# V stationary, the softmax's division in the transposing product, groups masked by one minimum

## What is computed

```python
x = x + xattn(layernorm(x), ctx, Wq, Wk, Wv, Wo, bo)
#   4 heads of 64: attn = softmax(q k^T / 8); (attn v) Wo^T + bo
x = x + ffn(layernorm(x), ...)
#   gate: scores = softmax(xf gw + gb), 32 experts in 8 groups of 4
#   a group's score is the sum of its 2 best; the 4 best groups stay,
#   the rest is masked; the 4 best experts of what stays get the token
#   routed experts (256 -> 128 -> 256, silu) and one shared expert
```

## Time and profile before

| | us |
|---|---|
| median of three runs | 429.52 |
| the three runs | 429.52, 421.88, 429.8 |
| the profiled execution | 428.41 |
| its span, first to last instruction | 426.6 |
| mean granted TensorE clock | 0.935 of full speed |
| PE, DVE, ACT, POOL busy | 343.8, 276.8, 183.5, 169.6 |

### The profile page before, as it was taken

One profiled execution on the slowest core, in us unless ns is written; L12 is line 12 of the kernel. 1 busy time (PEld: TensorE's weight loads), 2 busy tenths in 40 slices (PEclk: granted clock), 3 DMA queues, 4 the chain that ended last, 5 costly groups with the idle time before them and its releaser, 6 DMA issues.

```text
span 426.6 us, 8875 instructions
## 1 busy us (share of the span) xinstructions
PE 343.8 (81%) x2356; PEld 293.2 (69%) x2356; DVE 276.8 (65%) x906; ACT 183.5 (43%) x621; POOL 169.6 (40%) x197
## 2 busy tenths in 40 slices
PE   4889999999999899989697888889888778885000
PEld 3687988888879787768586866778777666673000
DVE  4736697786978869795423665556655565564297
ACT  2384675666657644441123444444444344342000
POOL 3702005362543625664300644554554534554000
PEclk9987999999999999997888999999999999999555
DMA  7992617557316412132121454554454534531699
GB/s 238 347 367 77 209 51 276 183 201 247 118 61 224 169 47 94 47 98 113 64 76 37 153 151 141 163 154 140 149 153 151 161 115 142 158 115 65 249 412 347
DMA packets 34277, 68.95 MB, mean 162 GB/s; under 512 B 5323, under 2 KB 25836, under 8 KB 33356
## 3 DMA queue, kind: packets, MB, share of 16 engines
q1 hardware_dynamic: 27292, 47.54, 35.0%
q0 software_dynamic: 6960, 21.11, 13.3%
HBM read 39.87 MB, written 28.77 MB: 161 GB/s over the span
## 4 chain that ended last, share of the span: by engine, by line
PE 43%; DVE 20%; issue 12%; ACT 7%; DMA 5%; DVEq 4%; another core or an unknown queue 4%; ACTq 2%; SPq 1%; POOL 0%; POOLq 0%
PE psS L1105 10%; PE psF L905 4%; PE psG L1114 3%; PE psS L1096 3%; PE psS L87 3%; PE psF L87 3%; DVEq L117 3%; DMA hs_ctx<-in_ctxT 2%; DVE nmax L1169 2%; PE psF L1114 2%; PE psF L1004 2%; DVE w L1565 2%; DVE xn2T_all L1553 2%; DMA w<-shares 2%
## 5 line engine op out<-in xcount | busy, mean ns | idle before, releaser
L609 POOL DMA_INDIRECT shares<-xn2T_all,e_number x81 | 84.0, 1036 | 104.3 <-DVE xn2T_all L1553 86.2
L568 POOL DMA_INDIRECT dispatch<-work,slot_now x64 | 62.4, 975 | 91.4 <-issue 47.8
L1105 PE MATMUL psS<-work,arena 128*128 128x128 f32 x648 | 87.6, 279 | 3.1 <-DVE arena L1548 2.8
L1105 PEld LDWEIGHTS psS<-work,arena 128*128 128x128 f32 x648 | 79.9, 194 | 4.8 <-DVE arena L1548 3.8
L1542 DVE SCALAR_TENSOR_TENSOR work<-psS,b,work 128x128 f32<-128x128 f32 x81 | 28.3, 349 | 62.0 <-issue 38.6
L806 ACT ACTIVATE work<-psS 128x256 f32<-128x256 f32 x81 | 30.9, 383 | 60.5 <-PE psS L1096 27.7
L1548 DVE COPY arena<-w 128x768 f32 x81 | 44.8, 554 | 6.7 <-PE psG L1114 2.9
L817 ACT ACTIVATE work<-psS,b 128x128 f32<-128x128 f32 x81 | 29.6, 366 | 36.9 <-PE psS L1105 34.1
L1114 PE MATMUL psG<-arena,work 128*128 128x256 f32 x80 | 25.9, 406 | 16.4 <-DVE work L1542 12.1
L1096 PE MATMUL psS<-ident,xn2T_all 128*128 128x128 f32 x162 | 31.8, 279 | 3.3 <-issue 1.5
L905 PE MATMUL psF<-arena 128*128 128x64 f32 x256 | 32.4, 282 | 1.3 <-ACT arena L682 1.3
(11 more groups left out here) (213 smaller groups left out, 754.7 us busy)
## 6 DMA issues: line engine op xcount, KB each, us to landing
xn2T_all<-dispatch SPq DMA_DIRECT2D x81, 160.0 KB
w<-in_w SPq DMA_DIRECT2D x6, 1536.0 KB, 8.4
w<-shares SPq DMA_DIRECT2D x7, 1024.0 KB, 11.2
dispatch<-padding SPq DMA_DIRECT2D x8, 640.0 KB
w<-in_w SPq DMA_DIRECT2D x1, 2304.0 KB, 8.0
out<-x SPq DMA_DIRECT2D x7, 256.0 KB, 10.1
hs_ctx<-in_ctxT SPq DMA_DIRECT2D x8, 192.0 KB, 3.4
x<-in_x SPq DMA_DIRECT2D x1, 1536.0 KB, 10.1
```

What stands on the lines that cost most here:

```text
L568: pool.indirect_dma_start(dispatch, bass.IndirectOffsetOnAxis(ap=slot_now[:, par, j * TOPK + k:j * TOPK + k + 1], axis=0), xn2[:, par, j, ...
L609: pool.indirect_dma_start(shares, bass.IndirectOffsetOnAxis(ap=e_number[:, u:u + 1], axis=0), e_y[:, u, :], None).then_inc(added[u], 16)
L1105: ins = pe.matmul(psS[:, 2 + u % 2, m * P:(m + 1) * P], e_w13[:, u % 3, k, m * INTER:(m + 1) * INTER], e_xT[:, u % 3, k, :], start=(k == 0 ...
```

## The change

The division by the row sums moves from behind the attention to before it. DVE makes, for each j, `scaling`: 4 diagonal blocks of 128 x 128, the identity times the reciprocals of one head's row sums. The product that turns the probabilities takes it in the identity's place, so pT comes out divided. attend then has V stationary (64 columns of it) and both j's pT as 256 moving columns; it writes the transposed result at once, the two heads of a bank half on two sets of partitions, the one on partitions 0 to 63, the other on 64 to 127. attend_T and attend_take are gone, and exps is split by j. `scaling` has one buffer: product 1 waits for probs_T 0. The router's keep, keep1 and two mask operations become `bound` = 7 - 2 rank and a minimum with the score. The order of the calls changes on PE, ACT and DVE, and the scatter is paced by other semaphores.

```diff
 def step(b, par, tail2):
     if tail2:
-        last_one = isinstance(b, int) and b == BATCHES - 1
-        scatter(b - 2, par, (("att_psum", TPB * (b + 1)),
-                             ("proj_psum", TPB * b + 1) if last_one else ("scores_psum", TPB * (b + 2)),
-                             ("proj_psum", TPB * (b + 1) if last_one else TPB * b + 1)))
+        last_two = isinstance(b, int) and b >= BATCHES - 2
+        last_one = last_two and b == BATCHES - 1
+        scatter(b - 2, par, (("attT_psum", b + 1) if last_one else ("scores_psum", TPB * (b + 2)),
+                             ("proj_psum", TPB * b + 1),
+                             ("proj_psum", TPB * (b + 1)) if last_two else ("q_psum", b + 3)))
 split_context(1, 1)
 step(0, 0, False)
...
-        ins.then_inc(s["probs_ready"], 1)
+def exps(b, j):
+    act.wait_ge(s["nmax_ready"], TPB * b + (j + 1))
+    for hp in range(HEADS):
+        ins = act.activation(probs[:, j, hp, :], psS[:, 2 * j + hp // 2, (hp % 2) * LQ:(hp % 2 + 1) * LQ], ACT.Exp,
+                             bias=nmax[:, j, hp:hp + 1], accum_out=psums[:, j, hp:hp + 1])
+    ins.then_inc(s["probs_ready"], 1)
 def gate_exps(b):
     act.wait_ge(s["gate_max"], b + 1)
...
     if front:
         q_out(b + 1)
         k_out(b + 1)
+    probs_out(b, 0)
+    if front:
         v_out(b + 1, 1 - par)
-    probs_out(b, 0)
     probs_out(b, 1)
     if tail:
         norm2_out(b - 1)
     if front2:
         round_context(b + 2, par, nth)
-    if tail:
-        gate_exps(b - 1)
-        norm2_keep(b - 1)
-    if front2:
         norm(b + 2)
     if not front:
+        if tail:
+            gate_exps(b - 1)
+            norm2_keep(b - 1)
         for c in range(WHOLE, 6):
             round_chunk(c)
         silu(0, 0)
         silu(0, 1)
     attend_out(b)
-    if not front:
+    if front:
+        exps(b + 1, 0)
+        if front2:
+            norm_out(b + 2)
+        if tail:
+            gate_exps(b - 1)
+            norm2_keep(b - 1)
+        exps(b + 1, 1)
+    else:
         silu(1, 0)
         silu(1, 1)
-    if front2:
-        norm_out(b + 2)
-    if front:
-        exps(b + 1)
 def norm2_out(b):
     act.wait_ge(s["xn2T_psum"], b + 1)
...
     if j == 0:
         pe.wait_ge(s["q_ready"], b + 1)
         pe.wait_ge(s["k_ready"], b + 1)
+        if not (isinstance(b, int) and b == 0):
+            pe.wait_ge(s["pT_ready"], TPB * (b - 1) + 1)
     for h in range(HEADS):
         r = HD * (h % 2)
         ins = pe.matmul(psS[:, 2 * j + h % 2, (h // 2) * LQ:(h // 2 + 1) * LQ], qT[r:r + HD, h // 2, j * P:(j + 1) * P],
...
     ins.then_inc(s["scores_psum"], 1)
 def probs_T(b, j):
-    pe.wait_ge(s["probs_ready"], TPB * b + (j + 1))
+    pe.wait_ge(s["scaling_ready"], TPB * b + (j + 1))
     for t in range(2):
         for hp in range(HEADS):
-            ins = pe.transpose(psS[:, 2 * j + t, hp * P:(hp + 1) * P], probs[:, j, hp, t * P:(t + 1) * P], ident[:, :])
+            ins = pe.matmul(psS[:, 2 * j + t, hp * P:(hp + 1) * P], probs[:, j, hp, t * P:(t + 1) * P], scaling[:, hp, :],
+                            start=True, stop=True)
     ins.then_inc(s["pT_psum"], 1)
-def attend(b, j, par, front):
-    pe.wait_ge(s["pT_ready"], TPB * b + (j + 1))
+def attend(b, par, front):
+    pe.wait_ge(s["pT_ready"], TPB * (b + 1))
     pe.wait_ge(s["v_ready"], b + 1)
     if front:
-        pe.wait_ge(s["q_ready" if j == 0 else "k_ready"], b + 2)
-    elif j == 1:
+        pe.wait_ge(s["k_ready"], b + 2)
+    else:
         pe.wait_ge(s["x1_ready"], TPB * b)
-    for hp in range(HEADS):
-        h = (hp % 2) * 2 + hp // 2
+    for k in range(KD):
+        y = psF[:, 1, k * LQ:(k + 1) * LQ].rearrange("p (j q) -> p j q", j=TPB)
         for t in range(2):
-            ins = pe.matmul(psF[:, 2 - j, h * HD:(h + 1) * HD], pT[:, j, t, hp, :], v_sb[:, par, t, h * HD:(h + 1) * HD],
-                            start=(t == 0), stop=(t == 1))
-    ins.then_inc(s["att_psum"], 1)
-def attend_T(b, front):
-    for j in range(TPB):
-        pe.wait_ge(s["att_ready"], TPB * b + (j + 1))
-        if front and j == 0:
-            pe.wait_ge(s["v_ready"], b + 2)
-        for k in range(KD):
-            ins = pe.transpose(attT_bank(b)[:, j * LQ + k * P:j * LQ + (k + 1) * P], att[:, j, k * P:(k + 1) * P], ident[:, :])
+            for r in range(2):
+                h, rows = 2 * k + r, slice(r * HD, (r + 1) * HD)
+                ins = pe.matmul(y[rows], v_sb[:, par, t, h * HD:(h + 1) * HD], pT[:, :, t, 2 * r + k, :],
+                                start=(t == 0), stop=(t == 1))
     ins.then_inc(s["attT_psum"], 1)
-def project(b):
+def project(b, front):
     pe.wait_ge(s["attT_ready"], b + 1)
+    if front:
+        pe.wait_ge(s["v_ready"], b + 2)
     for j in range(TPB):
         pe.matmul(proj_bank(b, j), part_rows[0:PARTS[-1] + 1, :], bo_parts[0:PARTS[-1] + 1, :], start=True, stop=False)
         for k in range(KD):
-            ins = pe.matmul(proj_bank(b, j), attT[:, j, k, :], wo[:, k, :], start=False, stop=(k == KD - 1))
+            ins = pe.matmul(proj_bank(b, j), attT[:, k, j * P:(j + 1) * P], wo[:, k, :], start=False, stop=(k == KD - 1))
         ins.then_inc(s["proj_psum"], 1)
 def norm2_T(b, par):
...
     if front:
         proj_q(b + 1)
         proj_k(b + 1, 1 - par)
+    probs_T(b, 0)
     if front:
         proj_v(b + 1, 1 - par)
-    probs_T(b, 0)
-    if not front:
+    else:
         pe.wait_ge(s["x1_ready"], TPB * (b - 1) + 1)
         shared_up(0, 0)
+    probs_T(b, 1)
     if tail2 and front:
         ranks(b - 2)
-    probs_T(b, 1)
     if not front:
         pe.wait_ge(s["pT_ready"], TPB * b + 1)
         shared_up(0, 1)
         ranks(b - 2)
     if tail:
         norm2_T(b - 1, 1 - par)
-    attend(b, 0, par, front)
+    if front:
+        scores(b + 1, 0)
+    attend(b, par, front)
     if tail:
         gate(b - 1)
-    attend(b, 1, par, front)
-    if front:
-        scores(b + 1, 0)
-    else:
-        shared_up(1, 0)
-    attend_T(b, front)
     if front:
         scores(b + 1, 1)
     else:
+        shared_up(1, 0)
         shared_up(1, 1)
     if front2:
         norm_T(b + 2)
-    project(b)
+    project(b, front)
 pe.wait_ge(s["wk_in"], 16)
 proj_k(0, 0)
...
-    dve.tensor_scalar(keep1[:, :, :], grank[:, :, :], TOPG - 0.5, 1.0, ALU.is_lt, ALU.subtract).then_inc(s["groups_kept"], 1)
+    dve.tensor_scalar(bound[:, :, :], grank[:, :, :], -2.0, 2.0 * TOPG - 1.0, ALU.mult, ALU.add).then_inc(s["groups_kept"], 1)
 def route_mask(b):
     dve.wait_ge(s["groups_kept"], b + 1)
-    st.did(dve.tensor_tensor(by_group(masked), by_group(score), spread(keep[:, :, :].rearrange("p t g -> p (t g)"), 2, GSIZE), ALU.mult), "kept")
-def route_others(b):
-    st.need("kept")
-    dve.tensor_tensor(by_group(masked), by_group(masked), spread(keep1[:, :, :].rearrange("p t g -> p (t g)"), 2, GSIZE),
-                      ALU.add).then_inc(s["masked_ready"], 1)
+    dve.tensor_tensor(by_group(masked), by_group(score), spread(bound[:, :, :].rearrange("p t g -> p (t g)"), 2, GSIZE),
+                      ALU.min).then_inc(s["masked_ready"], 1)
 def route_best(b):
...
     st.need("rows")
     dve.tensor_copy(slot_now[:, par, :], row_now[:, :, :].rearrange("p t k -> p (t k)")).then_inc(s["slots_ready"], 1)
-def attend_sums(b):
-    dve.wait_ge(s["probs_ready"], TPB * b + TPB)
-    st.did(dve.reciprocal(prcp[:, :, :], psums[:, :, :]), "prcp")
-def attend_take(b, j):
-    st.need("prcp")
-    dve.wait_ge(s["att_psum"], TPB * b + (j + 1))
-    dve.tensor_tensor(att[:, j, :].rearrange("p (h l d) -> p l h d", l=2, d=HD),
-                      psF[:, 2 - j, 0:D].rearrange("p (h l d) -> p l h d", l=2, d=HD),
-                      spread(prcp[:, j, :].rearrange("p (l h) -> p l h", l=2), 3, HD), ALU.mult).then_inc(s["att_ready"], 1)
+def attend_sums(b, j):
+    dve.wait_ge(s["probs_ready"], TPB * b + (j + 1))
+    st.did(dve.reciprocal(prcp[:, j, :], psums[:, j, :]), f"prcp{j}")
+def attend_scaling(b, j):
+    st.need(f"prcp{j}")
+    if not (isinstance(b, int) and b == 0 and j == 0):
+        dve.wait_ge(s["pT_psum"], TPB * b + j)
+    dve.tensor_tensor(scaling[:, :, :], spread(ident[:, :], 1, HEADS), spread(prcp[:, j, :], 2, P), ALU.mult).then_inc(s["scaling_ready"], 1)
 def rows_of(b, j):
     return x[:, ds(TPB * b + j, 1), :].rearrange("p a d -> p (a d)")
...
             residual(b, j)
         wait_apart(dve, s["x1_ready"], TPB * b + (j + 1))
         dve.bn_stats(st2[:, j, :], rows_of(b, j)).then_inc(stats_ready[j], 1)
-    if tail:
-        route_others(b - 1)
+    if attended:
+        attend_sums(b + 1, 0)
     for j in range(TPB):
         wait_apart(dve, stats_ready[j], nth)
         ins = dve.bn_aggr(mv2[:, j, :], st2[:, j, :])
...
         route_best(b - 1)
     st.need("aggr")
     rsqrt_var(n, mv2[:, :, 1])
+    if attended:
+        attend_scaling(b + 1, 0)
     if tail:
         route_index(b - 1)
     rsqrt_half(n)
...
         route_onehot()
     newton_wyy(n, tmp)
     newton_root(n, tmp)
```

(43 more changed lines are left out.)

8 lines of the change are left out of this document (1 added, 7 removed).

## The result

The changed kernel takes 451.69 us (median of 4 runs, 448.85 to 454.29), the kernel before on the same chip 428.52 (4 runs): ratio 1.063, 95% interval 1.046 to 1.081. Times are medians of all executions; ratios compare undisturbed executions alone, so that a ratio isn't exactly the quotient of two medians. The change makes the kernel slower, as forecast, but by 23 us and not by 9, and it lies above the whole range.

What follows compares the result with a forecast made beforehand. DVE's chain of waits, not PE, bounds the attention steps. 6.85 (five middle R to S), 1.94 + 0.3 (step 7), 0.9 (six S to R) and -0.3 (step 0) total +9.7 on 428.4 us: 438 us, range 431 to 449.

Steps and rivals of the forecast that it cites:

- The bound: Attention steps: a chain of waits mostly on DVE, not PE's 17.4 us of busy time, sets the 18.0 us step.
- S to R: From PE starting norm2_T (S) to DVE starting residual 0 (R), per step: 10.85 us against 10.70 before.
- PE's saving behind S: From S to R: the 2.4 us saved on PE are worth nothing, no step of the chain ending on them.
- The register work: DVE's register work for the next step, once hidden under maxima 1, now exposed: 0.25 us (none to 0.6).
- rival B: attend's column halves on PE don't overlap, so each attend ends 1.55 us later: 447 to 448 us; 15%.
- probs_T at 0.9 us: PE's turning of the probabilities, behind proj_k: probs_T(b, 0) takes 0.9 us and lands at R + 4.05.
- with 2.4 us less to do: PE's work per step falls by 2.4 us, so PE waits for residual 1 and 1.8 us before norm2_T.
- R to S: From DVE starting residual 0 to PE starting norm2_T: DVE's norm2 with router, 8.65 us against 7.28, +1.37.
- Rival C: PE's clock falls inside steps, up to 3.4 us a fall, one to three falls: 441 to 448 us; 10%.
- Step 0's norm2: Norm2 of step 0, which has no router: PE bounds it at 6.8 us, no change.
- The last step: R to S of step 7: probs_T starts at R + 3.0 behind scaling, 5.7 us follow; grows by 1.94.
- start: Step 0's attention up to project's end, with the clock falling again: about -0.3 us; without a fall -3.4.

Runs made afterwards that it cites:

- e8: The changed kernel with transposes in place of probs_T's products (division left out) and proj_q computed twice: 440.73 us, ratio 1.039.
- e5: The changed kernel without DVE's diagonals, probs_T's product multiplying by the identity (division left out): 441.31 us, ratio 1.044.
- e6: The changed kernel with transposes in place of probs_T's products and no diagonals (division left out): 411.62 us, ratio 1.021.
- the two paced ones: The changed kernel with GpSimd's last pair of indirect DMAs waiting for k_psum instead of q_psum, run twice: 426.26 us (1.050) and 427.60 us (1.067).
- e11: The changed kernel with ACT dividing the probabilities, PE transposing them, gate first, probs_T 0 before proj_k, indirect DMAs paced apart: 419.04 us, ratio 1.039.
- e7: The changed kernel with gate before attend on PE, gate_exps before attend_out on ACT, route_groups before maxima 1 on DVE: 438.26 us, ratio 1.034.
- e10: e7 with GpSimd's pairs of indirect DMAs paced apart: 408.98 us, ratio 1.014.
- e15: e7 unchanged, run again on another chip: 408.89 us, ratio 1.021.
- e16: e10 with, in the last step, shared_up(0, 0) ahead of probs_T 0 and ranks ahead of shared_up(0, 1): 407.28 us, ratio 1.017.
- e13: The changed kernel unchanged, run again on another chip: 428.78 us, ratio 1.066.

## Why the prediction was wrong in size

**The bound and S to R: right.** S to R changed by +0.4 over seven; six times 0.15 was forecast. gate_exps came where it was said to, and PE's saving behind S was worth nothing there, as said. The register work showed in one step only, at the end of a round of the loop: 0.61 us before R = 100.65, S to R 11.20; the other middle ones are 10.6, not 10.85. (The prediction's own terms give 10.7: 7.63 + 1.27 + 0.21 + 1.36 + 0.1 - 0.1 + 0.25.) Column halves do overlap (16 records in 1.95 us), so rival B is refuted. The Trainium skill (TensorE: Matmul & The Clock Gate, Part 3: Packing small matmuls) has weight loads overlap only where the row group differs, which gave an estimate of 0.85 us more an attend; these records do not show it, and here the measurement decides.

**The failed step: probs_T at 0.9 us.** The prediction took "probs_T(b, 0) takes 0.9" from the transpose and never priced the new product. It measured 1.8. That is two products a step, so "with 2.4 us less to do" became about 0.5 (-1.5 in attend, -0.8 attend_T, +1.8), and PE's row behind residual 1 ends at R+8.8 instead of R+7.1, past DVE's R+8.1. R to S at full clock became 9.5, not 8.65. The matmuls' records in the trace of before showed it: an f32 product leaves two (4 of scores: x8; 4 of proj_q: x8), a transpose one (8 of probs_T: x8). e8 has the forecast's 8.7 and less (8.25 to 8.81) with transposes, e5 the 9.24 without diagonals.

**The second: the clock.** Rival C had 10% and "one to three of them". That PE is "busy half the time and the clock stays 1.00" was a single window far away, and weighed too much. Falls hit three of the six R to S before the last in the changed kernel, and the last.

**Step 0's norm2: "no change"** was +1.8: PE bounds it, as said, and two products of 0.9 more are just that. e5 (8.41) and e6 (6.59, transposes and no diagonals) show it. **The last step: 1.94** was 6.7. The wait for the diagonal was sized right (R+3.09 for R+3.0); what follows it was to take 5.7 us. The two products add 1.8, and the clock, which fell in PE's wait of 5.2 us, stayed at 0.50 for the first 5.8 us of the work (167.4 to 173.2), by estimate another 2.9.

The sum, term by term, in us:

| term | forecast | measured |
|---|---|---|
| five middle R to S at full clock (5 x 9.5 less their 36.0 before) | 6.85 | 11.5 |
| step 0's R to S | 0 | 1.8 |
| falls of the clock in these six (61.3 less 8.4 less 47.5) | 0 | 5.4 |
| last R to S, with the 0.3 forecast behind it | 2.2 | 6.7 |
| S to R (six forecast, seven measured) | 0.9 | 0.4 |
| start | -0.3 | -0.2 |
| the rest behind the last S | 0 | -0.7 |
| together | 9.7 | 24.9 |

**What stays open.** Why a fall comes in one step and not in the next. Every profiled kernel that let PE stand 2 us before proj_k had falls in its steps, but the two paced ones had one between 55 and 160 us; their timed executions were no faster. Falls also came behind waits of 1.5 to 2.3 us before norm2_T (e8, e11). Where the gate went first and PE had no wait over 1 us, none of the four profiled executions (e7, e10, e15, e16) had a fall in steps 1 to 5. So the idle time goes with the falls; that it causes them was not isolated, since the gate's move changed the order too. What holds the semaphores back was not isolated either: the row of indirect DMAs goes with it, on some chips.

## What to carry to other kernels

Price a product by a product of the same type, never by a transpose of the same size: here, in f32, it takes twice the records and twice the time. An engine that is given less to do isn't freed by that; when its wait moves to one spot in front of the row that sets the end, the clock may pay for it, and the first thing to try is to move work into that spot. Here moving the gate brought 20 of the 27 us by which e13 lies above the kernel before, but 13 of them because another chain got shorter: split such a gain by stretch before you name its cause. Follow the row of the second engine to its end too: by the forecast's own numbers it was 1.0 us short of being the bound.
